# A two-layer graph network on one core: x's statistics ahead of the blocks' bounds, two small jobs handed to GpSimd, and shorter gathers for padding tiles

## What is computed

```python
h = relu(layernorm(x))
ef = (relu(ea @ We1 + be1) @ We2 + be2) * sigmoid(ew * Wt + bt)          # per edge
msg = relu(concat([h[src], ef]) @ Wn1 + bn1) @ Wn2 + bn2
x = x + segment_sum(msg, dst) + h                                         # layer 0
h = relu(layernorm(x))
g = h + segment_sum(h[src], dst)
x = x + relu(relu(g @ W1 + b1) @ W2 + b2)                                 # layer 1
```

## Time and profile before

| | us |
|---|---|
| median of 3 runs | 3589.09 (3583.87 to 3596.16) |
| the profiled execution's own time | 3590.76 |
| its span in the trace | 3589.0 |
| PE / DVE / POOL / ACT busy | 2681.7 / 1962.9 / 2068.4 / 1004.6 |
| prologue: start to the first use of the tiles' bounds | 0 to 64 |
| between the layers | 2594 to 2712 |

### The profile page before, as it was taken

One profiled execution on the slowest core, in us unless ns is written; L12 is line 12 of the kernel. 1 busy time (PEld: TensorE's weight loads), 2 busy tenths in 40 slices (PEclk: granted clock), 3 DMA queues, 4 the chain that ended last, 5 costly groups with the idle time before them and its releaser, 6 DMA issues.

```text
span 3589.0 us, 51735 instructions
## 1 busy us (share of the span) xinstructions
PE 2681.7 (75%) x14584; PEld 1614.4 (45%) x14585; DVE 1962.9 (55%) x4112; ACT 1004.6 (28%) x1000; POOL 2068.4 (58%) x2104
## 2 busy tenths in 40 slices
PE   4688878788777877788777877877745767666777
PEld 2444444444444444444434443433432544544554
DVE  7655655566565666566656666665763333233333
ACT  3233333333333333333333332322231111011111
POOL 4666666666566656666666566655324556555552
PEclk8788888788887887888888888888865766767778
DMA  5444444444343444344343443433222434334332
GB/s 188 110 124 134 130 132 126 128 127 135 121 127 122 126 122 123 121 126 123 122 124 124 122 123 121 124 106 118 48 94 84 152 99 129 104 111 126 117 103 62
DMA packets 229412, 426.77 MB, mean 119 GB/s; under 512 B 82703, under 2 KB 141584, under 8 KB 229072
## 3 DMA queue, kind: packets, MB, share of 16 engines
q0 software_dynamic: 74752, 153.23, 16.3%
q1 hardware_dynamic: 103152, 177.42, 15.0%
q10 hardware_dynamic: 51266, 93.34, 7.4%
HBM read 364.35 MB, written 59.43 MB: 118 GB/s over the span
## 4 chain that ended last, share of the span: by engine, by line
PE 41%; issue 20%; DVE 17%; another core or an unknown queue 11%; DVEq 9%; DMA 1%; SPq 0%; ACT 0%; ACTq 0%
PE ps L891 9%; PE ps L803 9%; PE ps L762 8%; PE ps L771 5%; DVE nodes L1152 5%; PE ps L782 4%; PE ps L754 3%; DVEq L1086 2%; DVEq L1132 2%; DVE arena L1152 2%; DVE hot L1107 1%; PE ps L881 1%; DVE acc L1094 1%; DVEq L1149 1%
## 5 line engine op out<-in xcount | busy, mean ns | idle before, releaser
L525 POOL DMA_INDIRECT big<-table,idx x2080 | 2044.2, 983 | 1391.8 <-issue 588.2
L803 PE MATMUL ps<-nodes 128*128 128x500 bf16 x1280 | 461.1, 476 | 348.7 <-issue 200.0
L762 PE MATMUL ps<-arena,we 128*128 128x512 f32 x784 | 516.4, 791 | 18.5 <-issue 13.3
L611 ACT ACTIVATE big<-big 128x1024 f32<-128x1024 f32 x196 | 207.1, 1057 | 1072.0 <-DVE big L1101 932.0
L782 PE MATMUL ps<-hot,big 128*128 128x64 f32 x3136 | 391.3, 274 | 99.4 <-issue 67.2
L1152 DVE TENSOR_SCALAR nodes<-iota_k,win_off,nodes 128x500 bf16<-128x500 f16 x1280 | 453.0, 405 | 0.0
L782 PEld LDWEIGHTS ps<-hot,big 128*128 128x128 f32 x3136 | 378.0, 194 | 102.2 <-issue 100.1
L1149 DVE TENSOR_TENSOR nodes<-iota_b,nodes 128x384 bf16<-128x384 f16 (+1 forms) x492 | 244.8, 497 | 278.6 <-remote 156.9
L803 PEld LDWEIGHTS ps<-nodes 128*128 128x128 bf16 x1280 | 107.6, 106 | 589.1 <-issue 308.0
L1101 DVE TENSOR_TENSOR big<-ps,big 128x1024 f32<-128x1024 f32 x196 | 239.0, 1219 | 225.5 <-issue 217.6
L601 ACT ACTIVATE arena<-ps,cols 128x1024 f32<-128x1024 f32 x196 | 218.6, 1115 | 405.3 <-PE ps L754 222.3
(11 more groups left out here) (139 smaller groups left out, 2512.4 us busy)
## 6 DMA issues: line engine op xcount, KB each, us to landing
arena<-in_ew SPq DMA_DIRECT2D x196, 512.0 KB
arena<-in_ea SPq DMA_DIRECT2D x196, 256.0 KB
counts_d<-arena ACTq DMA_DIRECT2D x192, 245.0 KB
acc<-counts_d ACTq DMA_DIRECT2D x15, 2940.0 KB
big<-table,idx POOLq DMA_INDIRECT x2080
table<-big SPq DMA_DIRECT2D x7, 672.0 KB, 3.0
idx<-in_src SPq DMA_DIRECT2D x260, 4.0 KB
xs<-in_x SPq DMA_DIRECT2D x7, 448.0 KB, 8.7
```

The costliest lines, as they stand in the source:

```text
L525: pool.indirect_dma_start(to(u, q, t), None, table, bass.IndirectOffsetOnAxis(ap=idx[:, u, at:at + 1], axis=0))\
L762: pe.matmul(p_ef[q], we2[:, :], hid[:, q, :], start=True, stop=True).then_inc(ef_mm, 1)
L803: m = pe.matmul(to, hots[:, t, :], keys[:, t, :], start=False, stop=True, skip_group_check=True)
```

## The change

Four edits:

1. SP loads x first, then `dst_b` and `dst_t`; it issues the first four pairs' loads (12 DMAs) before it waits for the bounds; it reads the loop counts later. DVE takes x's statistics first, then the bounds, and makes the loop counts (`sweep_params`, one instruction longer) after the sixth group of the node loop.
2. POOL adds the Relu into `xs` in the prologue; DVE doesn't.
3. Between the layers POOL makes the first bf16 part as well as the second; `left` has two buffers; DVE copies the transposes into `acc` in a loop of its own after all the parts.
4. The gathers of the five padding tiles fetch 16 rows, in both layers; POOL reads one loop count more ahead of layer 1's gathers.

```diff
@@ SP
-            sp.dma_start(dst_b, dst_blocks).then_inc(dst_loaded, 16)
             for g in range(NG):
                 sp.dma_start(xs[:, g * GT:(g + 1) * GT, :],
...
-                if g == 0:
-                    sp.dma_start(dst_t[:, :], dst_tiles).then_inc(dst_tiles_loaded, 16)
+            sp.dma_start(dst_b, dst_blocks).then_inc(dst_loaded, 16)
+            sp.dma_start(dst_t[:, :], dst_tiles).then_inc(dst_tiles_loaded, 16)
@@ GpSimd
-            pool.wait_ge(sweeps_made, 1)
-            sweeps, start, total, bodies = load_params(pool)
-
-            def gather_block(table, to, u, q, landed):
+            for g in range(NG):
+                x_g = xs[:, g * GT:(g + 1) * GT, :]
+                pool.wait_ge(normed, g + 1)
+                pool.tensor_tensor(x_g, x_g, stages[g % 2], ALU.add).then_inc(xh_made, 1)
+
+            def gather_block(table, to, u, q, landed, n=TB):
                 for t in range(TB):
                     at = q * TB + t
+                    rows_of = slice(0, P if t < n else 16)
                     pool.indirect_dma_start(
-                        to(u, q, t), None, table,
-                        bass.IndirectOffsetOnAxis(ap=idx[:, u, at:at + 1], axis=0))\
+                        to(u, q, t)[rows_of], None, table,
+                        bass.IndirectOffsetOnAxis(ap=idx[rows_of, u, at:at + 1], axis=0))\
                         .then_inc(landed[u][q], 16)
...
-            for g in range(NG):
-                pool.wait_ge(left_made, g + 1)
-                pool.tensor_copy(parts[:, g % 2, :, 1, :], left).then_inc(parts_second, 1)
+            for g in range(NG + 1):
+                if g < NG:
+                    pool.wait_ge(normed1, g + 1)
+                    if g >= 2:
+                        pool.wait_ge(table1_stored[g % 2], 16 * (g // 2))
+                    pool.tensor_copy(parts[:, g % 2, :, 0, :], nodes[:, g * GT:(g + 1) * GT, :]).then_inc(parts_first, 1)
+                if g >= 1:
+                    pool.wait_ge(left_made, g)
+                    pool.tensor_copy(parts[:, (g - 1) % 2, :, 1, :], lefts[(g - 1) % 2]).then_inc(parts_second, 1)
@@ ScalarE, in the loop over g between the layers
-                act.wait_ge(normed1, g + 1)
-                if g >= 2:
-                    act.wait_ge(table1_stored[g % 2], 16 * (g // 2))
-                act.activation(parts[:, g % 2, :, 0, :], nodes[:, g * GT:(g + 1) * GT, :], ACT.Copy).then_inc(parts_first, 1)
@@ VectorE, prologue
             for g in range(NG + 1):
                 if g < NG:
-                    x_g = xs[:, g * GT:(g + 1) * GT, :]
-                    dve.wait_ge(normed, g + 1)
-                    dve.tensor_tensor(x_g, x_g, stages[g % 2], ALU.add).then_inc(xh_made, 1)
                     dve.wait_ge(turned, g + 1)
...
+                if g == NG - 2:
+                    sweep_params()
@@ VectorE, between the layers
+            for g in range(NG + 1):
+                if g < NG:
+                    dve.wait_ge(parts_first, g + 1)
+                    if g >= 2:
+                        dve.wait_ge(parts_made, g - 1)
+                    dve.tensor_tensor(lefts[g % 2], nodes[:, g * GT:(g + 1) * GT, :], parts[:, g % 2, :, 0, :], ALU.subtract)\
+                       .then_inc(left_made, 1)
+                m = g - 1
+                if m >= 0:
+                    dve.wait_ge(parts_second, m + 1)
+                    dve.tensor_tensor(parts[:, m % 2, :, 2, :], lefts[m % 2], parts[:, m % 2, :, 1, :], ALU.subtract)\
+                       .then_inc(parts_made, 1)
             for g in range(NG):
-                dve.wait_ge(parts_first, g + 1)
-                if g:
-                    dve.wait_ge(parts_made, g)
-                dve.tensor_tensor(left, nodes[:, g * GT:(g + 1) * GT, :], parts[:, g % 2, :, 0, :], ALU.subtract)\
-                   .then_inc(left_made, 1)
                 dve.wait_ge(turned1, g + 1)
                 dve.tensor_copy(acc_group(g), p_turn[g % 2]).then_inc(acc1_made, 1)
-                dve.wait_ge(parts_second, g + 1)
-                dve.tensor_tensor(parts[:, g % 2, :, 2, :], left, parts[:, g % 2, :, 1, :], ALU.subtract)\
-                   .then_inc(parts_made, 1)
```

More of the change, by code:

```diff
@@ L204, in gnn_program @@
         parts = big[:, 0:2 * GT * D * NP3 // 2].bitcast(BF16).rearrange("p (s t i d) -> p s t i d", s=2, t=GT, i=NP3)
-        left = big[:, GT * D * NP3:GT * D * NP3 + GT * D].rearrange("p (t d) -> p t d", t=GT)
+        lefts = [big[:, i * GT * D:(i + 1) * GT * D].rearrange("p (t d) -> p t d", t=GT) for i in (NP3, NP3 + 1)]
         ef = sb("ef", [P, 2, BLK])
@@ L435, in _ @@
                   .then_inc(tile_ends_loaded, 16)
+            sp.wait_ge(sweeps_made, 1)
+            sweeps, start, total, bodies = load_params(sp)
             for b in range(1, NBODY):
@@ L543, in _, with gather_body @@
                 gather_pair(table0, to_rows, u, gathered)
-            def gather_body(b):
+            def gather_body(b, last=False):
                 for u in range(RING):
@@ L550, in gather_body @@
                     pool.sem_inc(pairs_begun, 1)
-                    gather_block(table0, to_rows, u, 0, gathered)
+                    gather = gather_rest if last and u == RING - 1 else gather_block
+                    gather(table0, to_rows, u, 0, gathered)
                     pool.wait_ge(agg_mm, b * RING + (u - 2))
                     pool.sem_inc(pairs_begun, 1)
-                    gather_block(table0, to_rows, u, 1, gathered)
+                    gather(table0, to_rows, u, 1, gathered)
             for b in range(1, NBODY):
-                gather_body(b)
+                gather_body(b, b == NBODY - 1)
+            pool.wait_ge(sweeps_made, 1)
+            sweeps, start, total, bodies = load_params(pool)
             with pool.If(sweeps > 1):
@@ L562, in _, with gather_pair1 @@
             pool.tensor_copy(keys1, keys0).then_inc(keys_moved, 1)
-            for g in range(NG):
-                pool.wait_ge(left_made, g + 1)
-                pool.tensor_copy(parts[:, g % 2, :, 1, :], left).then_inc(parts_second, 1)
+            for g in range(NG + 1):
[7 more added lines that the diff above has]
+                    pool.tensor_copy(parts[:, (g - 1) % 2, :, 1, :], lefts[(g - 1) % 2]).then_inc(parts_second, 1)
             for s in (0, 1):
                 pool.wait_ge(table1_stored[s], 16 * ((NG + 1 - s) // 2))
-            with pool.Fori(0, total) as b:
+            last = pool.value_load(params[0:1, 4:5], min_val=LBODY, max_val=MAX_SWEEPS * NBODY)
+            def gather_pair1(b, u, gather):
+                pool.wait_ge(slot1_free, b * RING + u + 1)
+                pool.wait_ge(idx1_loaded[u], b * 16 + 16)
+                pool.sem_inc(pairs_begun, 1)
+                for q in (0, 1):
+                    gather(table1, to_rows1, u, q, gathered1)
+            with pool.Fori(0, last) as b:
                 for u in range(RING):
-                    pool.wait_ge(slot1_free, b * RING + u + 1)
-                    pool.wait_ge(idx1_loaded[u], b * 16 + 16)
-                    pool.sem_inc(pairs_begun, 1)
-                    gather_pair(table1, to_rows1, u, gathered1)
+                    gather_pair1(b, u, gather_block)
+            for u in range(RING):
+                gather_pair1(last, u, gather_block if u < RING - 1 else gather_rest)
         @block.scalar
@@ L962, in _ @@
             chain(dve.memset(stats[:, :, :], 0.0))
-            dve.wait_ge(dst_loaded, 16)
-            by_tile = dst_b.rearrange("p j (t c) -> p j t c", t=TB)
-            chain(dve.tensor_reduce(tleast[:, :, :], by_tile, AX.X, ALU.min))
-            chain(dve.tensor_reduce(tgreat[:, :, :], by_tile, AX.X, ALU.max))
-            settle()
-            chain(dve.tensor_reduce(least[:, :], tleast[:, :, :], AX.X, ALU.min))
-            dve.tensor_reduce(great[:, :], tgreat[:, :, :], AX.X, ALU.max).then_inc(base_made, 2)
             def layer_norm_scales(which):
@@ L1001, in _ @@
             layer_norm_scales(1)
[L1004 to L1008 removed]
+            dve.wait_ge(dst_loaded, 16)
+            by_tile = dst_b.rearrange("p j (t c) -> p j t c", t=TB)
+            chain(dve.tensor_reduce(tleast[:, :, :], by_tile, AX.X, ALU.min))
```

82 lines of the change are left out of this document (46 added, 36 removed).

## The result

The changed kernel takes **3614.66 us** (median of 5, 3605.25 to 3626.81) against 3589.09 us (3583.87 to 3597.29) before on the same chip: ratio **1.0072**, 95% interval 1.0041 to 1.0103. That is +25.6 us; the forecast was +9.9 us with a range that ended at 3611. The profiled execution is the fastest of the five (3605.25, span 3603.4), so its trace shows only +14.5 us against the earlier trace rows.

The account below looks back on a forecast made before the run. No engine fills the chain (PE 41%, issue 20%); edits were priced in two serial stretches, prologue and between the layers, that everything else waits for. -8.1 + 18.5 - 0.5 = +9.9 us on 3589.1 gave 3599.0, range 3584 to 3611.

Parts of the forecast that it names:

- What releases layer 1's gathers: Between the layers: table1's last store and one more loop count (+0.6 us) release the gathers, which start 17.5 us later.
- Term 2: Between the layers, edit 3: 17.5 us from later gathers plus 1 for PE's trickle, +18.5 us; ends 0 and +31.
- The chain in Term 2: Between the layers: each table1 store waits for the one before, 7.2 us a group instead of 3.87, last store +16.9.
- The collision: DVE operations with two SBUF inputs and POOL's SBUF reads exclude one another: sweep_params +1.6 us, left and cast 2.0 together.
- rival A: No collision between casts and DVE's subtractions: cycle 6.3 us, last store +11, sum +3, 3592 us; 20%.
- The burst decides, not PE's start: Start of layer 1: PE runs short while gathers run; its pace returns about 5 us after the 32nd gather.
- rival B: Start of layer 1: PE isn't held by the burst, so Term 2 is 0 and the total 3580 us; 12%.
- Rival C: Start of layer 1: PE's late start counts in full, +31 - 8 = +23, 3612 us; 10%.
- Term 1: Prologue, edits 1 and 2: nodes complete at 46.4 instead of 54.50, -8.1 us; ends -10 and -5.
- Term 3: Edit 4, the padding tiles' gathers: nothing in layer 1, 0 to -1 in layer 0; -0.5 us.
- The sum: Whole kernel: -8.1 + 18.5 - 0.5 = +9.9 us on the median 3589.1, giving 3599.0.

Follow-up runs that it names:

- k4: The changed kernel, but DVE frees layer 1's slots right after the last third part, ahead of the copies, instead of PE: ratio 1.0051, +15.5 us against the kernel before.
- k1: The kernel before with edits 1 and 2, last gathers split off and loop count read as in edit 4, all 128 rows fetched: ratio 0.9995, -1.9 us.
- k3: The kernel before with edit 4 alone: ratio 0.9995, -2.4 us against the kernel before.
- k9: The changed kernel with the loop counts worked out behind the node loop instead of inside it: ratio 1.0070, +22.7 us against the kernel before.
- Sets 1 and 2: The first two of four groups of follow-up kernels, each measured on one chip beside the kernel before: that takes 2889.6 and 2890.6 us.
- sets 3 and 4: The last two of four groups of follow-up kernels, each measured on one chip beside the kernel before: that takes 3592.3 and 3596.9 us.
- r_after: The changed kernel, unchanged, run again where the kernel before takes 2890 us: ratio 1.0076, +21.5 us.
- k13: Kernel before with edits 1, 2, 4, counts behind node loop, dst_t loaded behind weights; 24 layer 1 gathers held until PE's first 98 products: ratio 1.0026, +1.7 us.
- k12_act: The changed kernel with POOL's and DVE's loop halves exchanged, three part buffers, slots freed early by DVE, ACT making the first part: ratio 0.9997, -0.3 us.

## Why the prediction was wrong

- **What releases layer 1's gathers: the step that failed.** I wrote that POOL, once past the stores, reads one loop count and "the gathers start 17.5 us later", and let the copies delay PE alone. They delay the gathers: PE frees the slots behind the seventh copy. In the kernel before the slots were free 4 us ahead of the last store's landing (the last copy ended at 64.9, and 2662.6 + 3.0 is 68.8 on that count), and moving the copies behind the parts turned it into the last one. Measured +24.0, and +25.4 for the whole of Term 2 instead of +18.5; with the slots freed earlier +15 (k4 against k1 and k3, which read the same loop count). I had asked of the moved copies who waits for their data, and not what stands behind them on PE's queue.
- **The chain in Term 2: right.** A round of 7.2 us forecast, 6.9 measured; last store +16.9 forecast, +15.0 measured. Removing it gave back 14 to 17 us.
- **The collision (rival A's opposite): right.** `left` 1.78 us instead of 1.09, the last cast 1.73 us instead of 0.93, the first operation of the loop counts 1.63 us instead of 0.56. In these rows the later one is held until the earlier is through, or nearly.
- **The burst decides, not PE's start (rivals B and C): right where the kernel takes 3590 us.** Pace back 5.1 us after the 32nd gather, +25.4 with gathers +24.0; +1.6 us with PE 10 us late and gathers on time. Where it takes 2890 us PE isn't held by the burst, as rival B had it, and the loss is there all the same, so B's step from there to 3580 was wrong too. Rival C's 3612 lies nearest to the measured time, by another mechanism.
- **Term 1, the prologue: mis-sized, -4.2 instead of -8.1.** The start of ACT was right, and the loop counts were in the sum: 3.6 + 0.15 + 1.6 = 5.35 us of DVE's time, measured 4.9, with their input there in time. Two other steps were too short. PE waited for the weights' last load and held up ACT, which was done at 38.8 instead of 37.2. And I gave the last product "about 1 us"; it took 3.29, at half the clock behind the idle time that the counts leave PE. The last addition ends 3.8 us late by that. k9 shows that even this is not the end: 7 us won there is lost again, most of it since the counts hold PE. In the medians the prologue alone is worth 1.9 us (-4.0 to +1.2, k1).
- **Term 3: right**, nothing that can be measured (forecast -0.5, k3 -2.4, interval -5.2 to +2.3).
- **The sum** with the measured stages is -4.2 + 25.4 = +21.2; the three medians say 21.5 to 28.6. My range ended at +22, near rival C with the full gain of the prologue; the two misses, 3.9 and 6.9 us, lie on the same side and use nearly all of it up. What the first measurement shows above the stages' sum, 4.4 us, is within the scatter of its median; without it the time would have fallen just inside the range, with the same step wrong.

The Trainium skill ("SBUF — State Buffer", Who interferes with whom) gives the exclusion as it was found here, and adds one thing that I overlooked: `tensor_scalar` can run in a mode that takes both ports and then blocks against any GpSimd instruction, while `tensor_tensor` contends with GpSimd's reads alone. The first row of the prologue above agrees: 1.08 us for a 49-column TENSOR_SCALAR that takes 0.19 late in the program, until POOL's memset (4.96 to 15.61) was through; the TENSOR_TENSORs ahead of it took 0.25 beside the same memset.

## What to carry to other kernels

When work is moved to the end of a stretch, list the signals that stand behind it on every engine, not only the readers of its data: a "buffers are free" signal placed there by convenience becomes the gate of the next stage. When one loop does step g and step g-1 on the same in-order engine, follow the two waits together: a wait for the store of g-2 ahead of the work that g-1 needs makes a chain of stores. And before moving an elementwise operation to GpSimd, count DVE's two-input operations beside it: here the two engines together were no faster than DVE with a GpSimd that does half as much.

## What the runs showed of the hardware

- **The same kernel takes 2890 or 3593 us, and the chip alone may not decide it.** Sets 1 and 2: 2889.6 and 2890.6 us; sets 3 and 4 and the first measurement: 3589 to 3597. Sets 2 and 3 stand on record with the same chip number. Granted clock 0.886 and 0.80. Where it takes 2890, PE runs through the burst of gathers. In k1_prologue:

```profile
2174.05 12.76 PE L910 MATMUL ps<-acc,nodes 128*128 128x120 f32 x98 [6.26 <-DVEq L1348]
```

  98 in 12.8 us, and the first window starts 25 us earlier (96.0 against 120.9), with gathers at the same place. The chain of waits there is POOL's gathers:

```profile
POOL 33%; PE 28%; issue 17%; DVE 12%; DVEq 5%; DMA 5%; SPq 1%; POOLq 0%; ACT 0%; ACTq 0%; PEldq 0%
```

  (r_after, by engine), where the same kernel's profile in the first measurement has PE 40%, issue 19%. Why is open. I didn't expect that a cost which sits in the gathers' start would come out the same, 21.5 and 25.6 us, on both.
- **Where it takes 3590 us, a long burst of indirect DMAs by GpSimd comes with a dry stretch on PE, and in k13 on DVE.** DVE did 3 operations and PE none in 33 us there, PE for want of DVE's keys. The Trainium skill ("Runtime: NRT & Kernel Launch", Instruction fetch mechanics) calls fetching mostly hidden; these rows disagree if it is fetching, which none of them proves.
- **PE's pace while it is dry:** in k12_act single matmuls 2.10 us apart at the end of the burst; in the changed kernel 24 in 33.4 us.
